# A new order of instructions in the edge loop of a graph network kernel, and a split moved from GpSimd to ScalarE and VectorE

## The chip, the cores and the metric

The kernel runs on one core of a Trainium2 chip. The metric is the device time of one execution in microseconds. The engines are TensorE (PE, its weight loads PEld), VectorE (DVE), ScalarE (ACT), GpSimd (POOL) and the queue of SyncE (SP). Each runs its own instructions in the order in which they are written, and waits on semaphores.

## The reference

```python
# x (1250, 512), edges: src, dst (20000,), edge_attr (20000, 64)
mish = lambda z: z * tanh(softplus(z))
xn = layernorm(x)
edge_feat = concatenate([xn[src], xn[dst], edge_attr], -1)
h = mish(edge_feat @ W1 + b1)                 # "lin1"
messages = mish(h @ W2 + b2)                  # "lin2"
agg = segment_sum(messages, dst, 1250)
u = mish(concatenate([xn, agg], -1) @ W3 + b3)
x = x + layernorm(xn + u @ W4 + b4) * gamma + beta
x = x + ffn(layernorm(x))                     # routed feed-forward, top 2 of 16 experts
```

The edges are sorted by destination.

## The kernel before

Four phases follow each other with a barrier between them: a prologue (from xn it makes two tables, `src_table` = xn·W1[:512] and `dst_table` = xn·W1[512:1024] + b1, in DRAM), the edge phase, the node phase and the feed-forward phase. Only the edge phase is changed. It treats the edges in 83 pairs of tiles of 128 edges.

Matrix products are made at single precision from two parts: an operand is rounded to fp32r ("hi") and the remainder ("lo") is kept beside it, and hi·hi, hi·lo and lo·hi are added in PSUM.

For each pair these things are done:

- SP loads the indices of the pair (`idx_sl`) and the edge attributes (`ea_sl`).
- GpSimd fetches the rows of `src_table` by an indirect DMA (L706, one for each tile) and adds the rows of `dst_table` to them by a second one (L696, one for each tile), into `gath`. It splits the attributes into hi and lo (L713, L715, `ea_hl`), and makes the lo part of the message (L721, `msg_lo`).
- TensorE transposes the attributes (L859) into bank 0 of the pair's half of `ps_1`, ScalarE copies that out as `eaT` (L757), TensorE transposes the gathered rows (L873) into all of `ps_1`, and adds the attributes' product (L877, L878): that is lin1.
- The first mish: ScalarE Exp (L738), VectorE min and add (L782, "inc1"), ScalarE Square (L746), Ln (L752), Exp (L763), VectorE (e - 1)·z from PSUM (L809), then the hi part `hTh` (L814) and the lo part `hTl` (L795).
- lin2: a bias (L831) and 16 products of `hTh` with W2 hi and lo, then 8 of `hTl` with W2 hi (L828), into `ps_2`.
- The second mish: ScalarE L743, VectorE L785 ("inc2"), ScalarE L749, L760, L766, VectorE L818, then `msg_hi` (L800) on VectorE and `msg_lo` (L721) on GpSimd.
- `dloc` (L806) and `onehot` (L802) on VectorE, four products of `onehot` with the message (L842, L843) on TensorE, and two additions to the block's sums (L793) on VectorE.

All this is a software pipeline. Step s runs, on every engine and in an order written out by hand, parts of several pairs: on VectorE inc1 of pair s, inc2 of s-2, the sums of s-4, `hTl` of s-1, `msg_hi` and `onehot` of s-3, `dloc` of s+2, then h and `hTh` of s and the message of s-2. On TensorE it is: sums of s-4, the 18 hi products of lin2 of s-1, the attribute transposes of s+1, the 8 lo products of s-1, the gathered transposes and lin1 of s+1. On GpSimd: the `dst_table` fetch of s+2, the `src_table` fetch of s+3, the attribute split of s+2, `msg_lo` of s-3. There are two buffers of `ps_1`, of `ps_2` and of the activations, three of `gath`, and the sums borrow the first two banks of a half of `ps_1`.

Of the kernel before, what the change touches and what calls it, by code (L numbers as in the profile page):

```python
# [12 lines left out]
F32R = mybir.dt.float32r  # L13
# [596 lines left out]
def edge_phase(nc, T):  # L610
# [5 lines left out]
    IN, GA, E2 = 4, 3, 2 * P  # L616

    ctx, sems = ExitStack(), []
    with ctx:
# [8 lines left out]
        ea_sl = sb("ea_sl", [P, IN, 2, EDIM])  # L628
        ea_hl = sb("ea_hl", [P, 2, 2, 2 * EDIM], F32R)
# [3 lines left out]
        act2 = sb("act2", [P, 3, 2, HID])  # L633
# [15 lines left out]
        names = ("ea_hi split dst_ready eaT_ps eaT_ready gath_read lin1_ps exp1 inc1 sq1 ln1 quot1 h_ready h_hi h_lo lin2_ps "  # L649
# [6 lines left out]
        def exists(q):  # L656
            return 0 <= q < PAIRS

        def loaded(sem_of_slot, slots_n, q, per_pair):
            return sem_of_slot[q % slots_n], (q // slots_n + 1) * per_pair  # L660

        def two_banks(k):
            return ps_1[:, k].rearrange("p d e -> p (d e)").rearrange("p (j n) -> p j n", j=2)
# [6 lines left out]
        @block.sync  # L670
        def _(sp):
            for s in range(FIRST, LAST + 1):
                q = s + 5
                if exists(q):
                    k = q % IN
                    if q >= IN:
                        sp.wait_ge(*loaded(both_gath, GA, q - IN, 32))
                        sp.wait_ge(S["split"], q - IN + 1)
                        sp.wait_ge(S["dst_ready"], q - IN + 1)
                    for j in range(2):  # L680
                        first = sp.value_load(start_i[0:1, q * 2 + j:q * 2 + j + 1], min_val=0, max_val=EDGES)
                        sp.dma_start(idx_sl[:, k, j, :], idx_scr[bass.ds(first, P), :]).then_inc(idx_in[k], 16)
                        sp.dma_start(ea_sl[:, k, j, :], ea_scr[bass.ds(first, P), :]).then_inc(ea_in[k], 16)
                if s == PAIRS - 3:
                    sp.wait_ge(*loaded(both_gath, GA, PAIRS - 1, 32))
                    sp.dma_start(w_raw[:], T["W3"].rearrange("(k p) n -> p k n", p=P)).then_inc(S["w3_in"], 16)

        @block.gpsimd
        def _(pool):
            for s in range(FIRST, LAST + 1):  # L690
                b = s + 2
                if exists(b):
                    k = b % GA
# [5 lines left out]
                g = s + 3
                if exists(g):  # L700
                    k = g % GA
                    pool.wait_ge(*loaded(idx_in, IN, g, 32))
                    if g >= GA:
                        pool.wait_ge(S["gath_read"], g - GA + 1)
# [11 lines left out]
                m = s - 3  # L716
                if exists(m):
                    pool.wait_ge(S["msg_hi_ready"], m + 1)
                    if m >= 2:
                        pool.wait_ge(S["sum_ps"], m - 1)  # L720
                    nc.gpsimd.tensor_tensor(msg_lo[:, m % 2], act2[:, m % 3], f32(msg_hi[:, m % 2]), ALU.subtract).then_inc(S["msg_lo_ready"], 1)  # L721
# [5 lines left out]
        def _(act):  # L727
            nc.scalar.preload_act_table_set(EXP_LN_SET)

            for s in range(FIRST, LAST + 1):  # L730
                q, g, n = s, s - 2, s + 1
                first, second = exists(q), exists(g)
                a1, a2 = act1[:, q % 2], act2[:, g % 3]
                if first:
                    act.wait_ge(S["lin1_ps"], q + 1)
                    if q >= 2:
                        act.wait_ge(S["h_lo"], q - 1)
                    nc.scalar.activation(a1, ps_1[:, q % 2], ACT.Exp).then_inc(S["exp1"], 1)  # L738
                if second:
                    act.wait_ge(S["lin2_ps"], g + 1)  # L740
                    if g >= 3:
                        act.wait_ge(S["msg_lo_ready"], g - 2)
# [1015 lines left out]
```

## Time and profile before

| | |
|---|---|
| median of 3 runs | 1415.14 us (1413.94 to 1417.71) |
| profiled execution: its time | 1416.24 us |
| its span, first to last instruction | 1414.6 us |
| prologue ends, first instructions of the edge loop | near 115 us |
| edge loop | near 115 to 1053 us |
| granted clock of TensorE, whole span | 0.933 |
| granted clock, 300 to 900 us | 1.00 |

In the profile, L followed by a number is a line of the kernel before. "Idle before" is idle time of an engine in front of an instruction, with the instruction that ended it. "Issue" stands for idle time for which the profile shows no releaser. The mean duration of an instruction contains what it was held up after its start. In the timeline the next instruction of an engine often starts some hundredths of a us before the one ahead of it ends.

### The profile page before, as it was taken

To read this page: it belongs to the slowest core of one execution; us is meant where nothing else is said; L and a number is where in the kernel's file an instruction comes from. 1 tells how busy PE (TensorE), PEld (TensorE's weight loads), DVE (VectorE), ACT (ScalarE), POOL (GpSimd) and SP (SyncE) were. 2 spreads that over 40 slices of the span, in tenths; PEclk is the share of its full clock that TensorE was granted. 3 is DMA by queue.
4 is the path that set the end of the run, shared out by engine and by line. 5 is a ranking of instruction groups with operands and counts; after the bars stand their busy time and mean duration, and the time that the engine had idled before them with its cause. 6 is when DMAs were issued, how large, how long until landed. Compare 5 with 4: busy or idle time off the path is not lost. (4 is left out here: it accounts for less than half of the span.)

```text
span 1414.6 us, 20672 instructions
## 1 busy us (share of the span) xinstructions
PE 1145.5 (81%) x5823; PEld 912.1 (64%) x5824; DVE 1108.9 (78%) x1627; ACT 852.9 (60%) x1061; POOL 913.7 (65%) x755
## 2 busy tenths in 40 slices
PE   0992888889889899899898889889838997559972
PEld 0671666777677677677677777767626775558861
DVE  3840579999999999999999999999864876743364
ACT  1311667777777777777777777777843543333341
POOL 1333788898888888889889889888431210454410
PEclk9996899999999999999999999999968997679965
DMA  5534554554554554455455455455210111634452
GB/s 145 200 116 98 117 107 96 109 114 96 107 111 101 102 111 106 98 111 110 98 109 112 96 110 113 96 106 108 81 38 23 37 44 44 189 106 131 127 164 101
DMA packets 113398, 148.00 MB, mean 105 GB/s; under 512 B 55389, under 2 KB 63980, under 8 KB 113225
## 3 DMA queue, kind: packets, MB, share of 16 engines
q0 software_dynamic: 40912, 101.69, 32.8%
q1 hardware_dynamic: 72377, 45.20, 11.6%
q8 instruction: 41, 0.67, 0.2%
q14 instruction: 52, 0.43, 0.1%
q10 hardware_dynamic: 16, 0.02, 0.0%
HBM read 136.29 MB, written 15.66 MB: 107 GB/s over the span
## 5 line engine op out<-in xcount | busy, mean ns | idle before, releaser
L696 POOL DMA_INDIRECT gath<-dst_table,idx_sl x166 | 283.8, 1709 | 49.7 <-issue 27.2
L828 PE MATMUL ps<-W2l,hTh 128*128 128x512 f32 x664 | 264.2, 398 | 0.0
L828 PE MATMUL ps<-W2h,hTh 128*128 128x512 f32 x664 | 263.5, 397 | 0.0
L721 POOL TENSOR_TENSOR msg_lo<-act,msg_hi 128x1024 fp32r<-128x1024 f32 x83 | 213.3, 2570 | 33.9 <-DVE msg_hi L800 33.9
L706 POOL DMA_INDIRECT gath<-src_table,idx_sl x166 | 171.6, 1034 | 76.7 <-issue 50.3
L806 DVE TENSOR_TENSOR dloc<-idx_sl,block_off 128x2 f32<-128x2 int32 x83 | 180.3, 2172 | 14.9 <-DMA idx_sl<-idx_scr 14.9
L828 PE MATMUL ps<-W2h,hTl 128*128 128x512 f32 x664 | 174.9, 405 | 0.4 <-DVE hTl L795 0.2
L828 PEld LDWEIGHTS ps<-W2l,hTh 128*128 128x128 f32 x664 | 125.7, 189 | 30.6
L828 PEld LDWEIGHTS ps<-W2h,hTh 128*128 128x128 f32 x664 | 126.0, 190 | 26.4
L793 DVE TENSOR_TENSOR agg<-agg,ps 125x512 f32 x166 | 112.9, 680 | 31.0 <-DVE agg L793 23.3
L746 ACT ACTIVATE act<-act 128x1024 f32<-128x1024 f32 x83 | 88.2, 1062 | 77.6 <-DVE act L782 77.6
L828 PEld LDWEIGHTS ps<-W2h,hTl 128*128 128x128 f32 x664 | 118.6, 188 | 24.1 <-DVE hTl L795 1.3
L831 PE MATMUL ps<-bias_r,minus_r 128*128 128x512 f32 x166 | 74.6, 449 | 59.5 <-DVE act L818 59.5
L809 DVE SCALAR_TENSOR_TENSOR act<-act,ps 128x1024 f32<-128x1024 f32 x83 | 100.3, 1208 | 24.8 <-ACT act L763 24.8
L842 PE MATMUL ps<-msg_hi,onehot 128*126 128x512 f32 x166 | 73.2, 441 | 48.5 <-DVE act L809 30.7
L738 ACT ACTIVATE act<-ps 128x1024 f32<-128x1024 f32 x83 | 85.3, 1028 | 39.3 <-PE ps L878 39.3
L818 DVE SCALAR_TENSOR_TENSOR act<-act,ps 128x1024 f32<-128x1024 f32 x83 | 101.4, 1221 | 3.1 <-ACT act L766 0.4
L795 DVE TENSOR_TENSOR hTl<-act,hTh 128x1024 fp32r<-128x1024 f32 x83 | 102.6, 1236 | 0.0
L757 ACT ACTIVATE eaT<-ps 128x256 fp32r<-128x256 f32 x83 | 32.1, 386 | 108.9 <-PE ps L859 108.9
L760 ACT ACTIVATE act<-act,half_col 128x1024 f32<-128x1024 f32 x83 | 94.8, 1143 | 0.1
L831 PEld LDWEIGHTS ps<-bias_r,minus_r 128*128 128x128 f32 x166 | 31.5, 190 | 98.0 <-DVE act L818 94.0
L752 ACT ACTIVATE act<-act,half_col 128x1024 f32<-128x1024 f32 x83 | 94.3, 1137 | 0.1
(315 smaller groups left out, 2852.2 us busy)
## 6 DMA issues: line engine op xcount, KB each, us to landing
f_w_raw<-in_L_ffn_w_dram SPq DMA_DIRECT2D x32, 512.0 KB, 4.6
ea_sl<-ea_scr SPq DMA_DIRECT2D x166, 32.0 KB
ea_scr<-in_edge_attr_dram POOLq DMA_DIRECT2D x1, 5000.0 KB, 20.6
w_raw<-in_L_gnn_W_dram SPq DMA_DIRECT2D x3, 1024.0 KB, 18.6
idx_sl<-idx_scr SPq DMA_DIRECT2D x166, 1.5 KB, 1.7
gath<-src_table,idx_sl POOLq DMA_INDIRECT x166, 4.2
gath<-dst_table,idx_sl POOLq DMA_INDIRECT x166, 5.2
x_raw<-in_x_dram SPq DMA_DIRECT2D x5, 500.0 KB
```

Of the source, the lines that this page charges most:

```text
L696: pool.indirect_dma_start(out=gath[:, k, j, :], out_offset=None, in_=dst_table[:, :], in_offset=bass.IndirectOffsetOnAxis(ap=idx_sl[:, b % ...
L706: pool.indirect_dma_start(out=gath[:, k, j, :], out_offset=None, in_=src_table[:, :], in_offset=bass.IndirectOffsetOnAxis(ap=idx_sl[:, g % ...
L721: nc.gpsimd.tensor_tensor(msg_lo[:, m % 2], act2[:, m % 3], f32(msg_hi[:, m % 2]), ALU.subtract).then_inc(S["msg_lo_ready"], 1)
L752: nc.scalar.activation(a1, a1, ACT.Ln, bias=half_col[:], scale=0.5).then_inc(S["ln1"], 1)
L760: nc.scalar.activation(a2, a2, ACT.Ln, bias=half_col[:], scale=0.5).then_inc(S["ln2"], 1)
L793: nc.vector.tensor_tensor(row, row, two_banks((a + 1) % 2)[0:NB, j, :], ALU.add).then_inc(S["summed"], 1)
L795: nc.vector.tensor_tensor(hTl[:, r % 2], act1[:, r % 2], f32(hTh[:, r % 2]), ALU.subtract).then_inc(S["h_lo"], 1)
L806: nc.vector.tensor_tensor(dloc[:, 2 * n:2 * n + 2], idx_sl[:, n % IN, :, 2], block_off[:, 2 * n:2 * n + 2], ALU.subtract).then_inc(S["dst_ ...
L809: nc.vector.scalar_tensor_tensor(out=act1[:, q % 2], in0=act1[:, q % 2], scalar=1.0, in1=ps_1[:, q % 2], op0=ALU.subtract, op1=ALU.mult).t ...
L818: nc.vector.scalar_tensor_tensor(out=act2[:, g % 3], in0=act2[:, g % 3], scalar=1.0, in1=ps_2[:, g % 2], op0=ALU.subtract, op1=ALU.mult).t ...
L828: return nc.tensor.matmul(ps_2[:, r % 2, j, :], part[:, r % 2, d, j * P:(j + 1) * P], weights[:, d, :], start=False, stop=last)
L831: nc.tensor.matmul(ps_2[:, r % 2, j, :], minus_r[:], bias_r[:, 1, :], start=True, stop=False)
```

## The change

The arithmetic of the results is the same. What differs:

- **Attributes.** SP loads each tile's attributes twice, side by side, into a wider `ea_sl` (four loads a pair, two before). `ea_hl` and the two GpSimd instructions are gone. TensorE transposes both copies at once; ScalarE rounds all 128 partitions to hi (`eaT`), and VectorE then replaces partitions 64 to 127 by PSUM minus hi (new instruction, `eaT_lo`, 256 columns).
- **lin2** of a pair is spread over two steps: the bias and hi products of tile 1, then of tile 0, in step r+1; the lo products of tile 1 and of tile 0 in step r+2, with the rest of lin1 between them.
- **Gathered transposes** are divided by bank: bank 0 (d = 0, 1) at the end of a step, bank 1 (d = 2, 3) at the start of the next, where lin1 follows. The wait on the sums before the attribute transposes is on the first tile alone, that on the second tile stands before bank 1.
- **VectorE's order** in step s: `onehot` (s-4), h (s-1), `dloc` (s+2), `hTh` (s-1), message (s-3), inc1 (s), first sum (s-4), `msg_hi` (s-3), inc2 (s-2), `hTl` (s-1), `eaT_lo` (s+1), second sum (s-4).
- **ScalarE's order**: last Exp of the second mish (s-3), Exp (s), Exp (s-2), Square and Ln (s), `eaT` copy (s+1), Square (s-2), last Exp (s), Ln (s-2).
- **GpSimd's order**: `dst_table` fetch (s+1, before it was s+2), `src_table` fetch (s+3), `msg_lo` (s-3).

```diff
-        ea_sl = sb("ea_sl", [P, IN, 2, EDIM])
-        ea_hl = sb("ea_hl", [P, 2, 2, 2 * EDIM], F32R)
+        ea_sl = sb("ea_sl", [P, IN, 2, 2 * EDIM])
...
-                        sp.dma_start(ea_sl[:, k, j, :], ea_scr[bass.ds(first, P), :]).then_inc(ea_in[k], 16)
+                        for half in range(2):
+                            sp.dma_start(ea_sl[:, k, j, half * EDIM:(half + 1) * EDIM], ea_scr[bass.ds(first, P), :]).then_inc(ea_in[k], 16)
...
-                b = s + 2
+                p = s + 1
...
-                if exists(b):
-                    k = b % 2
-                    pool.wait_ge(*loaded(ea_in, IN, b, 32))
-                    if b >= 2:
-                        pool.wait_ge(S["eaT_ps"], b - 1)
-                    nc.gpsimd.tensor_copy(ea_hl[:, k, :, 0:EDIM], ea_sl[:, b % IN]).then_inc(S["ea_hi"], 1)
-                    pool.wait_ge(S["ea_hi"], b + 1)
-                    nc.gpsimd.tensor_tensor(ea_hl[:, k, :, EDIM:2 * EDIM], ea_sl[:, b % IN], f32(ea_hl[:, k, :, 0:EDIM]), ALU.subtract).then_inc(S["split"], 1)
...
+            for s in range(FIRST, LAST + 1):
+                p, r, g, f, m, n, l = s, s - 1, s - 2, s - 3, s - 4, s + 1, s + 2
+                a1, h, a2, a3 = act1[:, p % 2], act1[:, r % 2], act2[:, g % A2], act2[:, f % A2]
...
+                if exists(m):
+                    add_sums(m, 0)
+                if exists(f):
+                    if f >= 2:
+                        dve.wait_ge(S["sum_ps"], f - 1)
+                    dve.wait_ge(S["msg_ready"], f + 1)
+                    nc.vector.tensor_copy(msg_hi[:, f % 2], a3).then_inc(S["msg_hi_ready"], 1)
+                if exists(g):
+                    dve.wait_ge(S["exp2"], g + 1)
+                    nc.vector.tensor_scalar(a2, a2, EXP_MAX, 1.0, ALU.min, ALU.add).then_inc(S["inc2"], 1)
+                if exists(r):
+                    dve.wait_ge(S["h_hi"], r + 1)
+                    nc.vector.tensor_tensor(hTl[:, r % 2], h, f32(hTh[:, r % 2]), ALU.subtract).then_inc(S["h_lo"], 1)
+                if exists(n):
+                    dve.wait_ge(S["eaT_hi"], n + 1)
+                    nc.vector.tensor_tensor(eaT[EDIM:, n % 2, :], ps_1[EDIM:, n % 2, 0, :], f32(eaT[EDIM:, n % 2, :]), ALU.subtract).then_inc(S["eaT_lo"], 1)
+                if exists(m):
+                    add_sums(m, 1)
...
+            for s in range(FIRST, LAST + 1):
+                p, n, r, g, m = s, s + 1, s - 1, s - 2, s - 4
+                if exists(p):
+                    if p >= 5:
+                        pe.wait_ge(S["summed"], (p - 4) * 2)
+                    gathered_bank(p, 1).then_inc(S["gath_read"], 1)
+                if exists(g):
+                    pe.wait_ge(S["h_lo"], g + 1)
+                    lo_tile(g, 1)
...
+                    pe.wait_ge(S["onehot_ready"], m + 1)
+                    pe.wait_ge(S["msg_lo_ready"], m + 1)
+                    pe.wait_ge(S["h_ready"], min(m + 4, PAIRS))
...
+                    hi_tile(r, 1)
...
+                    if n >= 5:
+                        pe.wait_ge(S["summed"], (n - 5) * 2 + 1)
...
+                if exists(n):
+                    pe.wait_ge(*loaded(both_gath, GA, n, 32))
+                    gathered_bank(n, 0)
```

`hi_tile` is the bias and 8 products, `lo_tile` 4 products, and `gathered_bank` 4 transposes. `add_sums(p, j)` is one addition of L793 with its register load and its waits on `sum_ps` and on the sum before it.

## Rows read from the trace of the kernel before

**Rows 1.** Windows: length, busy us (count) of PE, PEld, DVE, ACT, POOL, clock, DMA share, GB/s.
```profile
300.00:500.00 200.00, 178.39 (x893) 141.08 (x893) 193.15 (x208) 154.68 (x169) 177.74 (x133) 1.00 0.53 107
```

**Rows 2.** Groups, 300 to 900 us: shapes, count, busy us, mean ns, idle before.
```profile
L696 POOL DMA_INDIRECT gath<-dst_table,idx_sl x114 | 195.6, 1716 | 25.8 <-issue 18.6 <-PE ps L873 1.4
...
L806 DVE TENSOR_TENSOR dloc<-idx_sl,block_off 128x2 f32<-128x2 int32 x56 | 132.0, 2357 | 0.0
...
L706 POOL DMA_INDIRECT gath<-src_table,idx_sl x112 | 115.0, 1027 | 34.1 <-issue 34.1
...
L793 DVE TENSOR_TENSOR agg<-agg,ps 125x512 f32 x112 | 76.1, 679 | 15.4 <-DVE agg L793 14.8 <-issue 0.6
```

**Rows 3.** Timeline of one step, GpSimd and VectorE: start, duration (us), engine, line, operation.
```profile
598.20 1.82 POOL L696 DMA_INDIRECT gath<-dst_table,idx_sl  x1
...
606.06 2.58 POOL L721 TENSOR_TENSOR msg_lo<-act,msg_hi 128x1024 fp32r<-128x1024 f32 x1
...
606.30 2.36 DVE L806 TENSOR_TENSOR dloc<-idx_sl,block_off 128x2 f32<-128x2 int32 x1
...
608.58 1.21 DVE L809 SCALAR_TENSOR_TENSOR act<-act,ps 128x1024 f32<-128x1024 f32 x1
...
608.78 1.82 POOL L696 DMA_INDIRECT gath<-dst_table,idx_sl  x1
```

**Rows 4.** Timeline of GpSimd, 1008 to 1062 us.
```profile
1010.50 2.52 POOL L721 TENSOR_TENSOR msg_lo<-act,msg_hi 128x1024 fp32r<-128x1024 f32 x1 [7.70 <-DVE msg_hi L800]
...
1029.19 2.52 POOL L721 TENSOR_TENSOR msg_lo<-act,msg_hi 128x1024 fp32r<-128x1024 f32 x1 [5.79 <-DVE msg_hi L800]
...
1043.22 2.45 POOL L721 TENSOR_TENSOR msg_lo<-act,msg_hi 128x1024 fp32r<-128x1024 f32 x1 [2.87 <-DVE msg_hi L800]
```

**Rows 5.** Timeline of VectorE, 1008 to 1062 us.
```profile
1010.33 0.41 DVE L802 TENSOR_TENSOR onehot<-iota_n,dloc 128x252 fp32r<-128x252 f32 x1
...
1016.28 0.69 DVE L782 TENSOR_SCALAR act<-act 128x1024 f32<-128x1024 f32 x1
...
1017.48 0.68 DVE L793 TENSOR_TENSOR agg<-agg,ps 125x512 f32 x1
1018.37 0.69 DVE L793 TENSOR_TENSOR agg<-agg,ps 125x512 f32 x1 [0.21 <-DVE agg L793]
1018.98 1.22 DVE L795 TENSOR_TENSOR hTl<-act,hTh 128x1024 fp32r<-128x1024 f32 x1
1020.11 0.69 DVE L800 CAST msg_hi<-act 128x1024 fp32r<-128x1024 f32 x1
...
1029.35 1.22 DVE L818 SCALAR_TENSOR_TENSOR act<-act,ps 128x1024 f32<-128x1024 f32 x1
...
1043.38 2.83 DVE L776 TENSOR_TENSOR w1l_w3l<-w_raw,w1h_w3h 128x512 fp32r<-128x512 f32 x1
```

**Rows 6.** Timeline of TensorE and ScalarE in the step of rows 3.
```profile
605.68 2.11 PE L828 MATMUL ps<-W2h,hTl 128*128 128x512 f32 x8
...
607.62 1.03 PE L873 MATMUL ps<-ident,gath 128*128 128x128 f32 x8
...
608.42 0.36 PE L877 MATMUL ps<-eaT,Wch 128*128 128x256 f32 x1
...
609.33 0.28 PE L878 MATMUL ps<-eaT,Wcl 128*128 128x256 f32 x1
...
609.64 1.04 ACT L738 ACTIVATE act<-ps 128x1024 f32<-128x1024 f32 x1 [0.36 <-PE ps L878]
```

**Rows 7.** Line 721, 200 to 1000 us: durations min/median/max, first and last start.
```profile
L721 POOL TENSOR_TENSOR msg_lo<-act,msg_hi x75: 2503/2578/2590, 199.6 to 989.9; 128x1024 fp32r<-128x1024 f32 x75
```

**Rows 8.** Timeline of ScalarE, fifth and sixth step of the loop.
```profile
175.10 1.02 ACT L738 ACTIVATE act<-ps 128x1024 f32<-128x1024 f32 x1 [0.37 <-PE ps L878]
...
192.52 1.03 ACT L738 ACTIVATE act<-ps 128x1024 f32<-128x1024 f32 x1 [0.36 <-PE ps L878]
```

**Rows 9.** DMA issues, 300 to 900 us: count, median us from issue to landing.
```profile
gath<-dst_table,idx_sl POOLq DMA_INDIRECT x114, 5.2
```

More of the change, by code:

```diff
@@ L648, in edge_phase @@
         src_gath, both_gath = slots("src_gath", GA), slots("both_gath", GA)
-        names = ("ea_hi split dst_ready eaT_ps eaT_ready gath_read lin1_ps exp1 inc1 sq1 ln1 quot1 h_ready h_hi h_lo lin2_ps "
+        names = ("dst_ready eaT_ps eaT_hi eaT_lo gath_read lin1_ps exp1 inc1 sq1 ln1 quot1 h_ready h_hi h_lo lin2_ps "
                  "exp2 inc2 sq2 ln2 quot2 msg_ready msg_hi_ready msg_lo_ready onehot_ready sum_ps summed w3_in w3_hi w3_lo").split()
@@ L654, in edge_phase, with exists, loaded, sums @@
         FIRST, LAST = -5, PAIRS + 3
[L656 to L663, printed above, removed]
+        def exists(p):
+            return 0 <= p < PAIRS
+        def loaded(sem_of_slot, n, p, per_pair):
+            return sem_of_slot[p % n], (p // n + 1) * per_pair
+        def sums(p):
+            return ps_1[:, (p + 1) % 2].rearrange("p d e -> p (d e)").rearrange("p (j n) -> p j n", j=2)
         act_parts = {PAIRS: (7, 0, 1, 2), PAIRS + 1: (3, 4, 5, 6)}
@@ L698, in _ @@
                                                 compute_op=ALU.add).then_inc(both_gath[k], 16)
[L699 to L704, printed above, removed]
+                p = s + 3
+                if exists(p):
+                    k = p % GA
+                    pool.wait_ge(*loaded(idx_in, IN, p, 32))
+                    if p >= GA:
+                        pool.wait_ge(S["gath_read"], p - GA + 1)
@@ L716, in _ @@
[L716 to L721, printed above, removed]
+                                                in_offset=bass.IndirectOffsetOnAxis(ap=idx_sl[:, p % IN, j, 0:1], axis=0)).then_inc(src_gath[k], 16)
@@ L722, in _ @@
+                p = s - 3
+                if exists(p):
+                    pool.wait_ge(S["msg_hi_ready"], p + 1)
+                    if p >= 2:
+                        pool.wait_ge(S["sum_ps"], p - 1)
+                    nc.gpsimd.tensor_tensor(msg_lo[:, p % 2], act2[:, p % A2], f32(msg_hi[:, p % 2]), ALU.subtract).then_inc(S["msg_lo_ready"], 1)
                 for w in pool_parts.get(s, ()):
@@ L772, in _, with add_sums @@
         def _(dve):
-            def lo_parts(s):
+            def add_sums(p, j):
+                b = dve.value_load(block_i[0:1, p * 2 + j:p * 2 + j + 1], min_val=0, max_val=BLOCKS - 1)
+                row = agg[:, bass.ds(b, 1), :].rearrange("p a d -> p (a d)")
+                dve.wait_ge(S["sum_ps"], p + 1)
+                if p * 2 + j > 0:
+                    dve.wait_ge(S["summed"], p * 2 + j)
+                nc.vector.tensor_tensor(row, row, sums(p)[0:NB, j, :], ALU.add).then_inc(S["summed"], 1)
@@ L822, in _, with gathered_bank @@
         @block.tensor
         def _(pe):
-            for s in range(FIRST, LAST + 1):
-                n, r, m = s + 1, s - 1, s - 4
-                def lin2(j, d, part, weights, last=False):
-                    return nc.tensor.matmul(ps_2[:, r % 2, j, :], part[:, r % 2, d, j * P:(j + 1) * P], weights[:, d, :], start=False, stop=last)
-                def hi_tile(j):
-                    nc.tensor.matmul(ps_2[:, r % 2, j, :], minus_r[:], bias_r[:, 1, :], start=True, stop=False)
-                    for d in range(KC):
-                        lin2(j, d, hTh, W2h)
-                        lin2(j, d, hTh, W2l)
+            def gathered_bank(p, bank):
+                for d in (2 * bank, 2 * bank + 1):
+                    for j in range(2):
+                        ins = nc.tensor.matmul(ps_1[:, p % 2, d, j * P:(j + 1) * P], lhsT=gath[:, p % GA, j, d * P:(d + 1) * P], rhs=ident[:],
+                                               is_transpose=True, start=(d == 2 * bank and j == 0), stop=False, skip_group_check=True)
+                return ins
@@ new lines, in lin2, with hi_tile, lo_tile @@
+            def lin2(p, j, d, part, weights, last=False):
+                return nc.tensor.matmul(ps_2[:, p % 2, j, :], part[:, p % 2, d, j * P:(j + 1) * P], weights[:, d, :], start=False, stop=last)
+            def hi_tile(p, j):
+                nc.tensor.matmul(ps_2[:, p % 2, j, :], minus_r[:], bias_r[:, 1, :], start=True, stop=False)
+                for d in range(KC):
+                    lin2(p, j, d, hTh, W2h)
+                    lin2(p, j, d, hTh, W2l)
+            def lo_tile(p, j):
+                for d in range(KC):
+                    ins = lin2(p, j, d, hTl, W2h, d == KC - 1)
+                return ins
```

182 lines of the change are left out of this document (74 added, 108 removed).

## The prediction

> **What bounds the kernel now.** I read the page first (shares and slices), then the windows by stage, the groups and waits of 300 to 900 us, and last the timeline of one step, because the change is an order of instructions. The window row [rows 1] shows VectorE busy 193 of 200 us, TensorE 178 and GpSimd 178, at full granted clock. The step is the unit: GpSimd's first fetch starts at 598.20 and again at 608.78, 10.58 us later [rows 3]; over the whole loop line 721 starts 75 times between 199.6 and 989.9 us, a mean of 10.68 us, since some steps are longer [rows 7].
>
> The busy share of VectorE deceives. Its `dloc` is an instruction of 2 columns and takes 2.36 us on the mean, 132 us in 600 [rows 2]. The timeline says why: it starts at 606.30 and ends at 608.66, with GpSimd's `msg_lo`, which runs from 606.06 to 608.64 [rows 3]. It stands still until GpSimd is done. Other pairs show for whom this holds. Line 776, a subtraction of two SBUF operands of 512 columns, took 2.83 us beside the `msg_lo` of 1043.22 to 1045.67, while L818, which reads twice as many columns, one operand from PSUM, took 1.22 us inside the `msg_lo` of 1029.19 to 1031.71 [rows 4, 5]. So in this kernel an instruction of VectorE that takes both of its inputs from SBUF waits for a running instruction of GpSimd; one that reads PSUM and one SBUF tensor does not. Also, when `msg_lo` has been waiting for `msg_hi`, VectorE's next instruction gets in first: `onehot` started at 1010.33, `msg_lo` at 1010.50 took 2.52 [rows 4, 5].
>
> GpSimd is full as well: from its last instruction's end at 608.64 the next starts at 608.78 [rows 3], and its only idle time is the 0.3 us ahead of each fetch (34.1 us over 112) [rows 2]. The step before the change is thus one ring of VectorE work and of the GpSimd instruction that VectorE waits for.
>
> **The change, part by part.**
>
> *GpSimd.* It loses the attribute split, two instructions. Left are two `dst_table` fetches at 1.72, two `src_table` fetches at 1.03, four gaps of 0.3 [rows 2], less one, and `msg_lo` at 2.45 where little held it [rows 4], with its gap of 0.14 [rows 3]: 3.44 + 2.06 + 0.9 + 2.59 = 9.0 us a step. It will have slack and so reach `msg_lo` before `msg_hi` exists. `msg_lo` will start when VectorE gives it out. That is the point of the case.
>
> *VectorE.* It gains `eaT_lo`, 256 columns from PSUM. 512 columns of L793 took 0.69 us and 1024 of L818 1.22 [rows 5], so 256 take 0.41, start to start 0.33. It loses the wait of the second sum for the first (0.26 us: 14.8 us over 56 pairs) [rows 2], because the sums now stand apart. The block moves: behind `msg_hi` now come inc2 (0.60) and `hTl` (1.13), where `onehot` and `dloc` came. inc2 starts as `msg_hi` ends, ahead of GpSimd; then `msg_lo` takes its 2.4 us, and `hTl`, with two SBUF inputs, is held. `dloc` lost 608.58 - 606.30 = 2.28 us start to start, hardly any of it work, so `hTl` loses 2.2. If inc2 were held instead the sum is the same. The price of the block is not lower than before, and it lies in a worse place: `dloc` was waited for by nobody soon, while `hTl`, `eaT_lo` and the second sum come after it now, and TensorE waits for the last two to begin the next lin1.
>
> *TensorE and ScalarE.* The instruction counts are equal. TensorE no longer stops in front of the hi products; ScalarE's `eaT` copy no longer waits behind 18 hi products but behind 9.
>
> *SP.* Two more loads a pair. The pair's attributes are now wanted a step later than the first instruction for them was, so I cost this at nothing; what hides it is the five steps between the load and the transposes.
>
> *The ring after the change*, from the end of a lin1 (time 0). ScalarE's Exp starts 0.03 later (609.61 to 609.64) and takes 1.03 [rows 6]; inc1 starts at 1.1 and gives way at 1.7. TensorE meanwhile runs four lo products and four for the sums: eight took 605.68 to 607.62, 1.94 us [rows 6]. So the first sum can start after 1.94 plus a hand-over; for the second sum that is 0.26 [rows 2], for ScalarE 0.03 [rows 6]; I take 0.15 and have 2.1. From there start to start: sum 0.61, `msg_hi` 0.61, inc2 0.60 [rows 5]: 3.9. Block 2.2: 6.1. `hTl` 1.13: 7.25. `eaT_lo` 0.33: 7.6. Second sum 0.69: 8.25. TensorE: hand-over 0.03, bank 1 (half of 1.03) 0.52, four lo products 0.97, lin1 608.42 to 609.61, 1.19 [rows 6]: **10.95 us**. VectorE's work between second sum and inc1 (`onehot`, h, `dloc`, `hTh`, message) lies beside that stretch of TensorE and ends before the Exp does. Bounds of the step: 10.8 with 0.03 for the hand-over, 11.2 with 0.26 at both sums.
>
> Against 10.58 that is +0.37 us, over some 75 regular steps +28 us (bounds +17 and +46).
>
> The start-up gets shorter. In the first steps GpSimd stood waiting for its own `src_table` fetch to land, fell behind, and the fifth step took from 175.10 to 192.52, 17.4 us, 6.8 more than a regular one [rows 8]. Now two steps lie between the two fetches, and no split stands before `msg_lo`. I take -10 us, between -7 (this step alone) and -15 (the early steps, without `msg_lo`, too). The drain has the same order of work; 0, give or take 2.
>
> Sum: +28 - 10 = +18 on the profiled execution's 1416.2, that is 1434; the median of the runs lies 1.1 lower: **1433 us**.
>
> One rule of the Trainium skill speaks against the change on top of this. Its page "VectorE: DVE Perf Modes", section "Two Vector instructions with no wait between them", says that an instruction whose operands start in another group of 32 partitions than the last ones starts only when all earlier ones have finished. `eaT_lo` works on partitions 64 to 127 alone, and no instruction of the loop before does. By it the 0.09 us overlap of neighbours (1018.98 + 1.22 is 1020.20, the next starts at 1020.11 [rows 5]) would be lost twice a step: 11.1 instead of 10.95, some 13 us more, 1446. No trace here shows it.
>
> **The rivals.**
>
> *The other side: `msg_lo` comes late enough to miss `hTl`.* If GpSimd asks for the port only when `hTl` has begun, `msg_lo` runs beside `eaT_lo` and the second sum, which read PSUM (0.33 + 0.61 = 0.94 us), and holds only `onehot`, for 2.2 - 0.94 = 1.3 us. That is off the ring above. Then the ring is 10.95 - 2.2 = 8.75, GpSimd needs 9.0 plus a wait of some 0.4 for `hTl`, and TensorE's own work 178.4/200 x 10.58 = 9.4 [rows 1]: a step of 9.3 to 9.5, and 75 x 1.15 = 86 us saved, 1320. It keeps itself up once there, since GpSimd is then always late. It decides from the point where GpSimd ends its fetches after VectorE reaches `hTl`, 3.9 on the ring. By the sum `msg_lo` ends near 6.2, and the fetches 6.5 us later (9.0 less `msg_lo` at 2.45), at 12.75, which is 1.8 of the next ring; there GpSimd waits. For it: GpSimd would have to be 2.1 us late once. Against: the fetches of 300 to 900 us last 1.72 and 1.03 on the mean with gaps of 0.3 and little else [rows 2], and the first steps have no `msg_lo`, so GpSimd enters early. A mix (some stretches so) would land between 1340 and 1410.
>
> *The block does not hold `hTl` whole*, because inc2 or `hTl` slips in between pieces of `msg_lo`, or the ring's hand-overs are shorter. At a block of 1.8 the step is 10.55, no change in the loop, and the start-up leaves -10: 1405 to 1415.
>
> *The gathered rows come late.* The `dst_table` fetch starts one step later. On the ring GpSimd issues its second half near 6.3 + 2.0 = 8.3 of the step before, and it lands 5.2 us later [rows 9], at 13.5. TensorE asks after 18 hi products and two transposes, at 1.94 + 4.3 + 0.2 = 6.4 of the next step, 17.4. That is 3.9 us of slack; only beyond that does each us cost 75 us. Little speaks for it.
>
> **How the numbers follow.** The measurement tells about 0.3%, 4 us, from no change. Held `hTl` as worked out, slower: 0.6, its own range 1421 to 1450. The block partly missed or the start-up gaining more, 1405 to 1419: 0.18, of it 0.13 within 0.3%. GpSimd late, whole or in stretches, 1320 to 1405: 0.17. Gathers late, over 1450: 0.05. So faster 0.22, same 0.13, slower 0.65. The range from 1398 to 1450 leaves out most of the third case and the last.
>
> **What the profile after would show.** Right: `hTl` with a mean near 3.4 us instead of 1.24, `dloc` near 0.15; `msg_lo` near 2.85 us with idle time ahead of it that `msg_hi` ends, 1 to 2 us a step; TensorE idle before the bank 1 transposes for the second sum, about 1.5 us a step, and none before the hi products; steps of 10.95; no step of 17 us at the start. Wrong: `hTl` at 1.24 and `onehot` at 1.5 to 2 us with steps under 9.6 would be the first rival; steps ended by a landing of `gath` the third.

## The result, and the profile after

The changed kernel takes 1455.52 us (median of 4 runs, 1453.93 to 1463.38) against 1415.8 us for the kernel before (4 runs). The ratio is 1.029, 95% interval 1.025 to 1.033: slower, and by more than twice the +18 us that was predicted. The profiled execution took 1455.7 us, its span is 1454.1; that of before was 1414.6, so the account below has to explain +39.5 us.

Windows of the kernel after, with the columns of [rows 1]:

```profile
300.00:500.00 200.00, 170.28 (x852) 134.97 (x852) 184.61 (x214) 149.81 (x160) 163.03 (x89) 0.98 0.53 106
500.00:700.00 200.00, 171.86 (x849) 136.44 (x848) 182.73 (x211) 149.67 (x161) 161.13 (x90) 0.97 0.53 106
700.00:900.00 200.00, 169.93 (x851) 135.16 (x852) 183.23 (x215) 148.74 (x159) 162.26 (x89) 0.98 0.54 105
```

TensorE does less in the same 200 us (170 us busy, 178 before), and its granted clock is no longer 1.00.

Groups of the kernel after, 300 to 900 us, as in [rows 2]:

```profile
L696 POOL DMA_INDIRECT gath<-dst_table,idx_sl x106 | 216.5, 2042 | 23.9 <-issue 17.9
L811 DVE TENSOR_TENSOR hTl<-act,hTh 128x1024 fp32r<-128x1024 f32 x53 | 181.9, 3432 | 0.0
...
L713 POOL TENSOR_TENSOR msg_lo<-act,msg_hi 128x1024 fp32r<-128x1024 f32 x53 | 147.7, 2787 | 56.8 <-DVE msg_hi L805 56.8
...
L706 POOL DMA_INDIRECT gath<-src_table,idx_sl x107 | 123.1, 1150 | 32.6 <-issue 32.6
...
L769 DVE TENSOR_TENSOR agg<-agg,ps 125x512 f32 x107 | 73.6, 688 | 18.2 <-PE ps L867 16.6
L826 PE MATMUL ps<-ident,gath 128*128 128x128 f32 x424 | 69.5, 288 | 87.9 <-DVE eaT L814 87.9
...
L786 DVE TENSOR_TENSOR dloc<-idx_sl,block_off 128x2 f32<-128x2 int32 x53 | 8.1, 152 | 0.0
```

`hTl` (L811) now has a mean of 3432 ns, `dloc` (L786) of 152: the 2.3 us that one instruction stood still have moved to the other. GpSimd waits 56.8 us before `msg_lo` (L713), every time for `msg_hi`. TensorE waits 87.9 us over 53 steps before the gathered transposes (L826), for `eaT_lo` (L814).

One step of the kernel after in the timeline, the counterpart of [rows 3, 6]:

```profile
605.15 1.03 ACT L732 ACTIVATE act<-ps 128x1024 f32<-128x1024 f32 x1 [2.48 <-PE ps L856]
...
607.11 0.69 DVE L769 TENSOR_TENSOR agg<-agg,ps 125x512 f32 x1 [0.21 <-PE ps L867]
...
608.32 0.69 DVE L808 TENSOR_SCALAR act<-act 128x1024 f32<-128x1024 f32 x1
...
608.49 2.80 POOL L713 TENSOR_TENSOR msg_lo<-act,msg_hi 128x1024 fp32r<-128x1024 f32 x1 [0.74 <-DVE msg_hi L805]
...
608.92 3.44 DVE L811 TENSOR_TENSOR hTl<-act,hTh 128x1024 fp32r<-128x1024 f32 x1
...
611.42 2.39 POOL L696 DMA_INDIRECT gath<-dst_table,idx_sl  x1
...
612.40 0.43 DVE L814 TENSOR_TENSOR eaT<-ps,eaT 64x256 fp32r<-64x256 f32 x1
...
612.86 0.69 DVE L769 TENSOR_TENSOR agg<-agg,ps 125x512 f32 x1
...
612.97 1.28 PE L826 MATMUL ps<-ident,gath 128*128 128x128 f32 x8 [1.61 <-DVE eaT L814]
...
614.01 1.18 PE L831 MATMUL ps<-W2h,hTl 128*128 128x512 f32 x4
...
615.03 0.28 PE L855 MATMUL ps<-eaT,Wch 128*128 128x256 f32 x1
...
615.85 0.28 PE L856 MATMUL ps<-eaT,Wcl 128*128 128x256 f32 x1
...
616.17 1.03 ACT L732 ACTIVATE act<-ps 128x1024 f32<-128x1024 f32 x1 [2.44 <-PE ps L856]
```

Follow it from the end of lin1, 605.11 (the last L856 starts 604.83 and takes 0.28). `msg_lo` starts at 608.49, before `hTl`, which starts at 608.92 and ends at 612.36. `eaT_lo`, the second sum and TensorE follow, and the next Exp starts at 616.17, 11.02 us after the last. The hold has a back side too: GpSimd's next fetch, beside the rest of `hTl`, takes 2.39 us, the second one, after `hTl`, 1.71.

ScalarE's timeline of the kernel after: the first Exp of the first mish, for the first pair and for the fifth to seventh (the fifth and sixth stand in [rows 8] for the kernel before):

```profile
141.67 1.02 ACT L732 ACTIVATE act<-ps 128x1024 f32<-128x1024 f32 x1 [18.37 <-PE ps L856]
...
176.64 1.03 ACT L732 ACTIVATE act<-ps 128x1024 f32<-128x1024 f32 x1 [1.55 <-PE ps L856]
...
187.67 1.03 ACT L732 ACTIVATE act<-ps 128x1024 f32<-128x1024 f32 x1 [2.45 <-PE ps L856]
...
198.69 1.03 ACT L732 ACTIVATE act<-ps 128x1024 f32<-128x1024 f32 x1 [2.44 <-PE ps L856]
```

The step of 17.4 us is gone; the fifth and sixth steps take 11.03 and 11.02.

### The profile page after: what moved, and what is told of

It reads as the page before. It is cut to its first block and busy times, and to the rows that moved or that the text cites. A ratio compares the mean times of both kernels' runs of the same rounds, so it can differ in the third digit from the quotient of the medians.

```text
span 1454.1 us, 20838 instructions
## 1 busy us (share of the span) xinstructions
PE 1142.6 (79%) x5823; PEld 910.3 (63%) x5824; DVE 1126.4 (77%) x1710; ACT 862.0 (59%) x1061; POOL 884.2 (61%) x589
## 5 line engine op out<-in xcount | busy, mean ns | idle before, releaser
L696 POOL DMA_INDIRECT gath<-dst_table,idx_sl x166 | 334.5, 2015 | 38.2 <-issue 28.7
L713 POOL TENSOR_TENSOR msg_lo<-act,msg_hi 128x1024 fp32r<-128x1024 f32 x83 | 230.7, 2780 | 108.2 <-DVE msg_hi L805 108.2
L811 DVE TENSOR_TENSOR hTl<-act,hTh 128x1024 fp32r<-128x1024 f32 x83 | 280.3, 3377 | 0.0
L706 POOL DMA_INDIRECT gath<-src_table,idx_sl x166 | 190.3, 1146 | 88.6 <-issue 48.8
L826 PE MATMUL ps<-ident,gath 128*128 128x128 f32 x664 | 108.7, 289 | 148.9 <-DVE eaT L814 133.7
L826 PEld LDWEIGHTS ps<-ident,gath 128*128 128x128 f32 x664 | 71.8, 143 | 200.8 <-issue 166.6
L831 PE MATMUL ps<-W2h,hTl 128*128 128x512 f32 x664 | 194.8, 416 | 1.9 <-DVE hTl L811 1.9
L798 DVE TENSOR_SCALAR act<-act 128x1024 f32<-128x1024 f32 x83 | 57.8, 696 | 55.6 <-ACT act L732 55.6
L750 ACT ACTIVATE act<-act 128x1024 f32<-128x1024 f32 x83 | 87.4, 1053 | 4.4 <-DVE act L808 4.4
L727 ACT ACTIVATE act<-act 128x1024 f32<-128x1024 f32 x83 | 87.8, 1058 | 2.6
L740 ACT ACTIVATE act<-act 128x1024 f32<-128x1024 f32 x83 | 87.1, 1049 | 1.7 <-DVE act L798 1.7
```

Source lines behind the costliest of these rows:

```text
L713: nc.gpsimd.tensor_tensor(msg_lo[:, p % 2], act2[:, p % A2], f32(msg_hi[:, p % 2]), ALU.subtract).then_inc(S["msg_lo_ready"], 1)
L727: nc.scalar.activation(a3, a3, ACT.Exp, scale=-1.0).then_inc(S["quot2"], 1)
L811: nc.vector.tensor_tensor(hTl[:, r % 2], h, f32(hTh[:, r % 2]), ALU.subtract).then_inc(S["h_lo"], 1)
L826: ins = nc.tensor.matmul(ps_1[:, p % 2, d, j * P:(j + 1) * P], lhsT=gath[:, p % GA, j, d * P:(d + 1) * P], rhs=ident[:], is_transpose=True ...
L831: return nc.tensor.matmul(ps_2[:, p % 2, j, :], part[:, p % 2, d, j * P:(j + 1) * P], weights[:, d, :], start=False, stop=last)
```

## The experiments

Median step means the distance of ScalarE's first Exp of successive pairs, from the seventh pair on. For the kernel after it is 11.02 (mean 11.22), for the one before 10.59 (mean 10.68). Ratios are to the kernel before on the same chip. All experiments but the fourth start from the changed kernel.

**1. `msg_lo` behind `hTl`.** GpSimd also waits for `hTl` before `msg_lo`.

```diff
                     pool.wait_ge(S["msg_hi_ready"], p + 1)
+                    pool.wait_ge(S["h_lo"], min(p + 3, PAIRS))
```

> The changed kernel, with one more wait on GpSimd: msg_lo starts only when hTl of the step has ended. Theory (msg_lo holds hTl for 2.2 us, on the ring that sets the step of 11.02 us): msg_lo now runs beside eaT_lo and the second sum and holds onehot instead, which is off the ring; hTl falls to 1.24 us, onehot rises to 1.5 us or more, the step falls to 9.3 to 9.6 us, the time to 1325 to 1350 us. Rival (the step is set by the new order of TensorE and ScalarE or by the split that moved to VectorE): msg_lo starts 3.4 us later than it could, nothing is gained, the step stays at 11 us or grows, 1455 us or more.

1321.38 us, ratio 0.933 (0.931 to 0.935), median step 9.51, granted clock 1.00. Timeline of one step:

```profile
604.55 1.21 DVE L812 TENSOR_TENSOR hTl<-act,hTh 128x1024 fp32r<-128x1024 f32 x1
...
605.89 2.40 POOL L714 TENSOR_TENSOR msg_lo<-act,msg_hi 128x1024 fp32r<-128x1024 f32 x1 [0.42 <-issue]
...
606.85 1.71 DVE L779 TENSOR_TENSOR onehot<-iota_n,dloc 128x252 fp32r<-128x252 f32 x1
```

`hTl` is back at 1.21 us, and `msg_lo` holds only `onehot`. One wait more takes 134 us away. So what costs the time is where `msg_lo` falls, not its work; the first rival had the mechanism, the step and the time (9.3 to 9.5, 1320) right, and only its condition was not met by itself. The step came out as expected, the time a little under the range that went with it.

**2. `msg_lo` on VectorE**, behind inc2; GpSimd only fetches.

```diff
-                    nc.gpsimd.tensor_tensor(msg_lo[:, p % 2], act2[:, p % A2], f32(msg_hi[:, p % 2]), ALU.subtract)
...
+                    nc.vector.tensor_tensor(msg_lo[:, f % 2], a3, f32(msg_hi[:, f % 2]), ALU.subtract).then_inc(S["msg_lo_ready"], 1)
```

> The changed kernel, with msg_lo computed by VectorE behind inc2 and nothing but fetches left on GpSimd. Theory of the held hTl: 2.2 us of block leave the ring and 1.13 us of work come in, step 11.02 - 1.1 = 9.9 us, about 1370 us. Rival (VectorE has too much to do, whoever works beside it): its work rises by 1.13 us, so the step rises to about 12 us and the time to about 1540 us.

1350.34 us, ratio 0.953 (0.951 to 0.955), median step 9.94, clock 1.00. `msg_lo` takes 1211 ns there and `hTl` 1216. Without GpSimd's instruction nothing is held: the step is 1.08 us shorter although VectorE does 1.2 us more, which is about what a hold of 2.2 us on the ring leaves. The step is the expected one; the time is 20 us under what was expected with it.

**3. `eaT_lo` on partitions 0 to 63**, so that no instruction of VectorE's loop starts in another partition.

```diff
-nc.vector.tensor_tensor(eaT[EDIM:, n % 2, :], ps_1[EDIM:, n % 2, 0, :], f32(eaT[EDIM:, n % 2, :]), ALU.subtract)
+nc.vector.tensor_tensor(eaT[0:EDIM, n % 2, :], ps_1[0:EDIM, n % 2, 0, :], f32(eaT[0:EDIM, n % 2, :]), ALU.subtract)
```

> The changed kernel, with the subtraction of the attributes done on partitions 0 to 63 in place of 64 to 127: the same size, but its operands start where those of its neighbours start. It makes the lo part in the wrong half, so the output is another one; the work is equal. Theory (VectorE starts an instruction early, before its neighbour has ended, only when the operands start in the same partitions; eaT_lo and the sum behind it each lost 0.1 us): eaT_lo and the sum start 0.09 us before the end of the one ahead, step 10.8 us, 15 us off, 1440 us. Rival (the gaps come from the waits in front of these instructions): no change, 1455 us.

1436.28 us, ratio 1.013 (1.011 to 1.015), median step 10.88, mean 10.99. (Both halves meet the same weights, so the sum is the same.) VectorE's timeline:

```profile
601.09 3.44 DVE L811 TENSOR_TENSOR hTl<-act,hTh 128x1024 fp32r<-128x1024 f32 x1
604.45 0.41 DVE L814 TENSOR_TENSOR eaT<-ps,eaT 64x256 fp32r<-64x256 f32 x1
604.78 0.67 DVE L769 TENSOR_TENSOR agg<-agg,ps 125x512 f32 x1
```

`eaT_lo` starts 0.08 us before the end of `hTl` (604.53), the sum 0.08 before the end of `eaT_lo`. In the kernel after they start 0.04 and 0.03 after it. Two overlaps are lost there, 0.12 and 0.11 us by these lines; the median step shows 0.14 of it. The rest of the 19 us lies mostly in the long steps, of which this run has four over 12 us and not seven.

**4. The kernel before, with `dloc` as VectorE's last instruction of a step**: its block comes away from `dloc`, nothing else is changed.

```diff
-                if exists(n):
-                    dve.wait_ge(*loaded(idx_in, IN, n, 32))
-                    nc.vector.tensor_tensor(dloc[:, 2 * n:2 * n + 2], ...)
...
                 lo_parts(s)
+                if exists(n):
+                    dve.wait_ge(*loaded(idx_in, IN, n, 32))
+                    nc.vector.tensor_tensor(dloc[:, 2 * n:2 * n + 2], ...)
```

> The kernel before, with dloc moved from in front of h to the end of VectorE's step, behind the message, so that msg_lo runs beside h, which reads PSUM. Theory: in the kernel before, the block of 2.2 us lay in a stretch where VectorE would have waited for ScalarE's last Exp anyway (it ended at 608.33, h began at 608.58), so it cost only some 0.2 us a step: step 10.36 us, 15 to 20 us off, about 1398 us. Rival (the block costs its whole length wherever it stands): 8.4 us a step or TensorE's 9.4, 1320 us.

1396.86 us, ratio 0.986 (0.984 to 0.989), median step 10.38. The group of h, 300 to 900 us:

```profile
L806 DVE SCALAR_TENSOR_TENSOR act<-act,ps 128x1024 f32<-128x1024 f32 x58 | 70.8, 1221 | 109.2 <-ACT act L763 109.2
```

VectorE is no longer held, and now stands idle for 1.88 us a step (109.2 over 58), for ScalarE's Exp. Of 2.3 us that `dloc` stood still, 0.2 us had been on the path. The place of a hold decides its price: the same 2.3 us cost nearly nothing in front of h, and all of it in front of `eaT_lo` and the second sum.

**5. TensorE's idle time filled.** Five products with a zero matrix behind the last hi product; they add nothing to the result. (`zero_r` is a new tile of zeros, made once before the loop; that part of the edit is left out here.)

```diff
                     hi_tile(r, 0)
+                    for _ in range(5):
+                        nc.tensor.matmul(ps_2[:, r % 2, 0, :], zero_r[:], W2h[:, 0, :], start=False, stop=False)
```

> The changed kernel, with five products of a zero matrix added by TensorE behind the hi products, into the stretch of 1.6 us in which it waits for eaT_lo (5 x 0.234 = 1.17 us of it). They add zero to the result. Theory (the seven steps of over 12 us in the changed kernel are steps in which TensorE had been idle for some 1.9 us and was then granted the lower clock, 1.7 us lost in each): the regular step stays at 11.0 us, the granted clock between 300 and 900 us is 1.00 in place of 0.97 and 0.98, no step is over 12 us, the time falls by about 12 us to 1443 us. Rival (the long steps come from something else, fetches or the loading of instructions): they stay, 1455 us or a little more.

1441.13 us, ratio 1.018 (1.015 to 1.021), median step again 11.02, mean 11.05, none over 12. Windows, middle stretch:

```profile
500.00:700.00 200.00, 191.69 (x961) 152.51 (x960) 187.72 (x218) 153.19 (x164) 166.85 (x91) 1.00 0.54 108
```

More work, 14 us less time. It acts on the long steps alone, by the clock (next section).

**6. Experiment 1, and h before `onehot`** on VectorE, so that h, which reads PSUM, is what runs beside `msg_lo`.

```diff
+                    pool.wait_ge(S["h_lo"], min(p + 3, PAIRS))
...
-                    nc.vector.tensor_tensor(onehot[:, m % 2], ..., ALU.is_equal)
                     nc.vector.scalar_tensor_tensor(out=h, in0=h, scalar=1.0, in1=ps_1[:, r % 2], ...)
+                    nc.vector.tensor_tensor(onehot[:, m % 2], ..., ALU.is_equal)
```

> As e1 (msg_lo waits for hTl), and on VectorE h comes before onehot, so that h, which reads PSUM, lies beside msg_lo too. Theory: beside the 2.4 us of msg_lo now lie 0.33 + 0.61 + 1.13 = 2.1 us of work that it does not hold; onehot falls from 1.71 to some 0.7 us, VectorE gets 1 us of slack and TensorE, at about 9.2 us of work, sets the step: 9.3 us in place of 9.51, about 1305 us. Rival (in e1 the step is set by TensorE already): no change, 1321 us.

1324.51 us, ratio 0.936 (0.933 to 0.938), median step 9.64: missed by 0.3 us a step. VectorE did become free (176 of 200 us), but it was not what set the step any more. GpSimd is idle for 57.7 us in front of `msg_lo`, over 63 steps. The profile names no releaser; the only wait that was added there is the one on `hTl`. Its fetches so start later, and TensorE's weight loads wait 18.9 us for their rows.

**7. One late `msg_lo`.** The wait of experiment 1 for one pair only.

```diff
+                    if p == 5:
+                        pool.wait_ge(S["h_lo"], p + 3)
```

> The changed kernel, with the extra wait of e1 on GpSimd for one pair alone (the sixth). Theory of two self-holding orders: once msg_lo has come late, GpSimd stays busy until after hTl has begun, and the steps stay at 9.5 us without any further wait; its margin is small (in e1 GpSimd ends its fetches some 0.35 us after hTl begins), so a delay of VectorE of over 0.35 us puts it back to steps of 11.02 us. I expect some 5 to 30 short steps after the sixth pair, and 1410 to 1448 us. Rival (the order does not hold itself): one short step and 1454 us. If it holds through: 1321 us.

1430.99 us, ratio 1.011 (1.007 to 1.014). After the one wait come eleven steps of 9.0 to 9.3 us without any further push, then one of 13.9, then 11.0 again to the end. Timeline of the last short step and of the one that falls back:

```profile
317.59 1.02 POOL L706 DMA_INDIRECT gath<-src_table,idx_sl  x1 [0.30 <-issue]
...
317.70 1.21 DVE L813 TENSOR_TENSOR hTl<-act,hTh 128x1024 fp32r<-128x1024 f32 x1
...
318.63 2.53 POOL L715 TENSOR_TENSOR msg_lo<-act,msg_hi 128x1024 fp32r<-128x1024 f32 x1
...
326.78 1.05 POOL L706 DMA_INDIRECT gath<-src_table,idx_sl  x1 [0.30 <-issue]
...
327.51 3.82 DVE L813 TENSOR_TENSOR hTl<-act,hTh 128x1024 fp32r<-128x1024 f32 x1
...
327.83 2.40 POOL L715 TENSOR_TENSOR msg_lo<-act,msg_hi 128x1024 fp32r<-128x1024 f32 x1
```

In the short step GpSimd ends its last fetch at 318.61, when `hTl` has run for 0.91 us, so `hTl` is not held. In the next round VectorE waits 0.40 us for its first sum, `msg_hi` takes 0.90 and not 0.69 beside a fetch, and `hTl` comes 0.6 us later against GpSimd. `msg_lo` follows its fetch 0.32 after `hTl`'s start, and `hTl` takes 3.82. The short order keeps itself up, as the rival said, until VectorE slips by 0.6 us. The slip alone does not decide the matter: experiment 9 meets the same one and goes on. The long order is the firmer one: in the kernel after, all 53 instructions of `msg_lo` from 300 to 900 us waited for `msg_hi`, so that it never left it.

**8. Experiment 6, with one attribute load** for both copies (a source that repeats) in place of two. TensorE's wait on the loads counts to 32 and no longer to 64 (left out here).

```diff
-                        for half in range(2):
-                            sp.dma_start(ea_sl[:, k, j, half * EDIM:(half + 1) * EDIM], ea_scr[bass.ds(first, P), :]).then_inc(ea_in[k], 16)
+                        sp.dma_start(ea_sl[:, k, j, :].rearrange("p (h e) -> p h e", h=2),
+                                     ea_scr[bass.ds(first, P), :].unsqueeze(1).to_broadcast([P, 2, EDIM])).then_inc(ea_in[k], 16)
```

> As e6, with both copies of a tile's attributes brought by one load whose source is read twice, in place of two loads. Theory (the two more loads of a pair delay the first index loads on SP's queue): the first Exp of the loop comes some 2 us earlier after the first index load than in e6, the steps stay, the time falls by 1 to 3 us. Rival (more small loads slow the fetches in every step): the time falls by more than 5 us.

1322.74 us, ratio 0.934 (0.932 to 0.937), median step unchanged at 9.64. From the first index load to the first Exp it takes 22.54 us, against 24.60 in experiment 6. That looks like the 2 us that were expected, but it is not shown to come from the loads: the eight kernels with two loads take between 22.96 us (experiment 1) and 24.60, and the same edit on experiment 9 (experiment 10) changes 23.51 to 23.77. What is shown is that the extra loads cost the regular step nothing.

**9. `msg_lo` behind inc2.** GpSimd waits for inc2, not for `hTl`.

```diff
                     pool.wait_ge(S["msg_hi_ready"], p + 1)
+                    pool.wait_ge(S["inc2"], min(p + 2, PAIRS))
```

> The changed kernel, with msg_lo waiting for inc2 of the step in place of hTl's end (e1). Theory: hTl starts as inc2 ends, before GpSimd's wait is over, so msg_lo comes second and starts the moment hTl gives way, without the 0.4 us in which GpSimd stood idle in e1; in e7 the steps in which GpSimd came by itself behind the start of hTl took 9.2 to 9.3 us. Step 9.25 us, about 1300 us. Rival (GpSimd's request, when it comes within some 0.3 us of hTl's start, still goes first, as in the step of e7 that took 13.92 us): hTl is held, steps of 11 us, 1455 us.

1303.19 us, ratio 0.920 (0.919 to 0.922), median step 9.28. Its window, the group of `msg_lo`, and a step in the timeline:

```profile
300.00:500.00 200.00, 199.00 (x1035) 160.80 (x1035) 196.74 (x259) 181.15 (x194) 176.88 (x108) 1.00 0.65 128
```

```profile
L714 POOL TENSOR_TENSOR msg_lo<-act,msg_hi 128x1024 fp32r<-128x1024 f32 x65 | 168.4, 2591 | 4.9 <-DVE msg_hi L806 2.0 <-DVE act L809 1.9
```

```profile
605.69 1.02 POOL L706 DMA_INDIRECT gath<-src_table,idx_sl  x1 [0.30 <-issue]
...
605.80 1.21 DVE L812 TENSOR_TENSOR hTl<-act,hTh 128x1024 fp32r<-128x1024 f32 x1
...
606.73 2.54 POOL L714 TENSOR_TENSOR msg_lo<-act,msg_hi 128x1024 fp32r<-128x1024 f32 x1
...
608.10 1.45 DVE L779 TENSOR_TENSOR onehot<-iota_n,dloc 128x252 fp32r<-128x252 f32 x1
```

In a regular step no wait ends anything: GpSimd arrives by itself behind the start of `hTl` (606.73 against 605.80). Over the whole loop the new wait is what ended GpSimd's idle time four times: before the first `msg_lo`, at 168.53, and before three of the last ones, where GpSimd has no `src_table` fetch left to do, as at 894.18:

```profile
894.18 3.27 POOL L714 TENSOR_TENSOR msg_lo<-act,msg_hi 128x1024 fp32r<-128x1024 f32 x1 [1.94 <-DVE act L809]
```

This one took 3.27 us, so GpSimd was held and not `hTl`. (The 2.0 us put down to `msg_hi` are those of the step before, where `msg_lo` started at 885.00, 0.14 us after inc2's end as well.) In between, `msg_lo` came only 0.33 to 0.35 us behind the start of `hTl` five times. The second of these is the very step in which experiment 7 fell back, the 17th `msg_lo`:

```profile
317.58 1.21 DVE L812 TENSOR_TENSOR hTl<-act,hTh 128x1024 fp32r<-128x1024 f32 x1
...
317.90 3.13 POOL L714 TENSOR_TENSOR msg_lo<-act,msg_hi 128x1024 fp32r<-128x1024 f32 x1
```

VectorE waits 0.39 us for its first sum (0.40 there), `msg_hi` takes 0.91 us, and `msg_lo` follows its fetch 0.32 us after `hTl`'s start. But now `hTl` runs through and GpSimd is held, and the short order goes on. The wait on inc2 ended no idle time in this step (inc2 was over at 317.65). All 86 meetings at 0.33 to 0.36 us in experiments 9 to 11, which have that wait, went this way; the one without it, in experiment 7, went the other. Whether the wait decides it although it is already met, or chance did in experiment 7, is not shown. TensorE is busy 199 of 200 us.

**10. Experiment 9 with one attribute load**, that is the diffs of experiments 9 and 8 together.

> As e9, with one load in place of two for a tile's attributes, as in e8. By e8 against e6: 2 us less at the start, equal steps; 1 to 3 us below e9.

1299.46 us, ratio 0.918 (0.916 to 0.919), median step 9.23: the fastest kernel of this study, 156 us under the change as it was made and 116 under the kernel before. The time from the first index load to the first Exp is no shorter than in experiment 9 (23.77 and 23.51 us); in the profiled executions the difference lies between the first and the last Exp (756.3 and 758.8 us).

**11. Experiment 10 with h before `onehot`**, the second part of the diff of experiment 6.

> As e10, with h before onehot on VectorE as in e6. Theory (in e6 it was GpSimd, told to wait for the end of hTl and standing idle for 0.4 to 1.0 us, and its late fetches that set the step, so that VectorE's slack was worth nothing): now TensorE with its 9.2 us of work sets it, 9.2 us a step, level with e10 or up to 5 us below. Rival (the order itself is worse: the late onehot or the early h costs something on TensorE): over 9.5 us as in e6.

1315.3 us, ratio 0.929 (0.927 to 0.930), median step 9.48: slower, where I expected it level or faster. `hTl` and `msg_lo`:

```profile
606.05 1.21 DVE L812 TENSOR_TENSOR hTl<-act,hTh 128x1024 fp32r<-128x1024 f32 x1
...
606.40 3.12 POOL L714 TENSOR_TENSOR msg_lo<-act,msg_hi 128x1024 fp32r<-128x1024 f32 x1
```

Here `msg_lo` starts 0.35 us after `hTl` and takes 3.12 us: now GpSimd is the one held, and its own ring (3.12, fetches of 1.68, 1.55, 0.99 and 1.06, gaps of 0.15 and three times 0.3: 9.45) sets the step.

## Why the prediction went wrong

**The step that failed** is the price of the idle time that the change gives TensorE: the prediction counted its length, as a part of the ring, and put what it does to TensorE's clock at nothing. That is 11.8 of the 21.4 us missed. The other misses, worked out below, are the time until the first Exp (6.3 us), put at nothing, and a regular step that was 0.07 us too short.

**The mechanism was right.** `msg_lo` goes first, `hTl` is held whole (3432 ns, "near 3.4"), `dloc` is at 152 ns, `msg_lo` at 2787 ns ("near 2.85"), GpSimd waits for `msg_hi`, TensorE waits before bank 1 of the transposes (1.61, "about 1.5"), and no step of 17 us is left. Experiments 1 and 9 show that the order of these two instructions makes the difference between 11.02 and 9.3 to 9.5 us. GpSimd's wait was over-estimated: it is 0.74 us in the regular step ("1 to 2" was forecast; the mean of 1.07 takes in the long steps), because its fetches take longer than in the kernel before (means 2042 and 1150 ns, not 1716 and 1027). GpSimd so misses the first rival's order by 1.2 us, not by the 2.1 of the prediction: its fetches end at 607.75, and `hTl` starts at 608.92. The releaser was named wrongly: TensorE stops already in front of bank 0, at its own wait for `eaT_lo`, which the prediction had overlooked. It costs nothing beyond, since the second sum frees bank 1 when bank 0 is done.

**The ring, term by term**, from the end of lin1 in the step above:

| | predicted | measured |
|---|---|---|
| first sum starts | 2.1 | 2.00 |
| `hTl` starts | 3.9 | 3.81 |
| `eaT_lo` starts | 7.25 | 7.29 |
| second sum starts | 7.6 | 7.75 |
| lo products start | 8.8 | 8.90 |
| lin1 starts | 9.75 | 9.92 |
| lin1 ends | 10.95 | 11.02 |

The largest error is the start of the second sum, 0.46 behind `eaT_lo` and not 0.33. This is the rule that the prediction set aside, and experiment 3 confirms it: 11.02 falls to 10.88 once all instructions start in the same partition, with the same waits in front of them. The Trainium skill's page "VectorE: DVE Perf Modes", section "Two Vector instructions with no wait between them", says that of such an instruction and of the one behind it; the trace agrees with it in both places.

**The account of the 39.5 us.** The first Exp's line, of the kernel before and after (durations, then first and last start):

```profile
L738 ACT ACTIVATE act<-ps x83: 1024/1027/1038, 135.3 to 1014.4; 128x1024 f32<-128x1024 f32 x83
```

```profile
L732 ACT ACTIVATE act<-ps x83: 1010/1027/1028, 141.7 to 1051.5; 128x1024 f32<-128x1024 f32 x83
```

| | predicted | measured |
|---|---|---|
| until the first Exp | 0 | +6.3 |
| first six steps | -10 | -10.5 |
| regular steps, 76 x 0.433 (75 x 0.37) | +28 | +32.9 |
| seven steps of 12.3 to 12.9 us | 0 | +11.8 |
| other irregular steps (6.9 before, 3.5 after) | 0 | -3.4 |
| after the last Exp | 0 | +2.4 |
| sum | +18 | +39.5 |

Half of what was missed is one term that the prediction had not at all: **TensorE's clock**. It foresaw TensorE's idle time of 1.5 us a step and gave it no price beyond its length. Windows of the kernel after around one long step, and TensorE's timeline in it:

```profile
402.00:405.80 3.80, 1.91 (x9) 1.20 (x7) 3.74 (x3) 3.77 (x5) 3.64 (x2) 1.00 0.16 38
405.80:410.40 4.60, 4.55 (x21) 3.96 (x22) 3.94 (x6) 0.45 (x1) 3.69 (x4) 0.63 0.58 93
410.40:412.00 1.60, 1.60 (x9) 1.30 (x8) 0.35 (x1) 1.41 (x2) 0.88 (x1) 1.00 0.93 219
```

```profile
405.85 1.38 PE L826 MATMUL ps<-ident,gath 128*128 128x128 f32 x8 [1.94 <-DVE eaT L814]
406.89 2.05 PE L831 MATMUL ps<-W2h,hTl 128*128 128x512 f32 x4
```

After 1.94 us of idle time the granted clock is 0.63 over 4.6 us, so it is at the lower level, 1.2 GHz, for some three quarters of them (1.00 and 0.5 mixed). Four lo products take 2.05 us and not 1.18, and this step 12.92 us. Experiment 5 fills the idle time: the clock is 1.00, no step exceeds 12 us, and 14 us are gone with the regular step as it was. The idle time is thus shown to be the cause of the long steps. What decides in which of them the clock falls is not: the seven have between 1.67 and 1.94 us of idle time before the gathered transposes, and others with 2.02 and 2.04 us kept 1.00 (the first is a step of 11.47 us from 342.14).

**Until the first Exp** the prediction costed SP's extra loads at nothing, with five steps of cover. In the steady state that held (experiment 8 leaves the step as it was). Before the first pair there is no cover: from the first index load to the first Exp it is 24.44 us against 20.73 (20.84 in experiment 4, which has the same start). The doubled loads may be a part of these 3.7 us, and GpSimd's new order of fetches another; no run separates them. Experiment 8 took 2.1 us off with one load, experiment 10 nothing, and kernels with the same start differ by 1.6. The remaining 2.6 us lie ahead of the loop, where nothing was changed: over all kernels of this study the first index load starts between 113.8 and 118.5 us.

**The range** reached up to 1450 and ended there for want of the clock term: with the idle time filled, in experiment 5, the kernel takes 1441.13 us, inside it. By the chances the direction was right.

What stays open: why GpSimd's `msg_lo`, 0.32 us behind `hTl`'s start, holds it in experiment 7, while at the same distance it is itself held in experiments 9 to 11; the 3.7 us before the first Exp; and the 0.3 us that experiment 6 stands above its sum.

## What to carry to other kernels

When a long instruction of one engine holds another engine's instructions, ask first which of them it will meet after a change, and who waits for those: moving the meeting was worth 150 us here, with no work added or removed. Two orders can each keep themselves up, and it matters in which one a kernel starts. One early wait brought the fast one here but did not keep it (experiment 7); a wait in every step, which ends nothing in a regular one, was worth 152 us (experiment 9). An idle time of TensorE that a prediction introduces needs a price for the clock as well as its own length.

## What the runs showed of the hardware that was not expected

- The hold goes both ways. `hTl` beside a `msg_lo` that came first takes 3.43 us, not 1.21; GpSimd's fetch beside the rest of `hTl` 2.39, not 1.57 as in experiment 9 (at 609.42), where `hTl` is over by then; and `msg_lo`, when `hTl` is first, 3.12, not 2.40. The Trainium skill's "GPSIMD Engine Reference", section "Key points", names the contention with instructions of two SBUF inputs, without a size; the traces agree, and show that an instruction loses nearly all the time that the other still has to run.
- Five useless products a step made the kernel 14 us faster.
- One DMA whose source repeats is as good as two DMAs in the steady state (median step 9.64 both ways, experiments 6 and 8). That it is quicker at the start is not shown.
- The two engines' order of start does not settle who is held: at 0.32 us behind `hTl`'s start `msg_lo` held it once (experiment 7) and was held by it in the same step of experiment 9.
